# Counts product behind the last tile's heads product, first expert rows ahead of exponentials, and late token rows held back on GpSimd

## The reference

```python
x = x + tanh(g_xattn[0]) * L0_xattn(layernorm(x), ctx)      # 16 heads of 8
x = x + tanh(g_ffn[0])   * L0_ffn(layernorm(x))             # 8 experts, best 2 of each token
x = x + tanh(g_xattn[1]) * L1_xattn(layernorm(x), ctx)
x = x + tanh(g_ffn[1])   * L1_ffn(layernorm(x))             # quantized

def L0_ffn(x):
    probs = softmax(x @ router_w.T)
    topk_probs, topk_idx = top_k(probs, 2)                  # normalised to sum 1
    h = gelu(x @ w_fc[e] + b_fc[e])                         # for each chosen expert e
    y = sum over the two of topk_probs * (h @ w_proj[e] + b_proj[e])
```

## Time and profile before

| | us |
|---|---|
| median of 3 runs | 860.49 |
| lowest, highest run | 856.09, 864.86 |
| profiled execution, its device time | 855.35 |
| its span, first to last instruction | 853.6 |

### The profile page before, as it was taken

The page is one execution under the profiler, slowest core; times in us unless marked ns, Lnnn a source line. Parts: engine busy times, 40 slices in busy tenths (PEclk is TensorE's granted clock), DMA queues, the critical chain, the costliest instruction groups (busy, mean ns, idle before and its releaser), DMA issues. The chain is left out here.

```text
span 853.6 us, 19514 instructions
## 1 busy us (share of the span) xinstructions
PE 696.7 (82%) x6608; PEld 539.2 (63%) x6608; DVE 720.7 (84%) x1821; ACT 595.1 (70%) x1210; POOL 580.8 (68%) x561
## 2 busy tenths in 40 slices
PE   5988879999999989898989989999926879256535
PEld 2767657787877767776768777777723657122234
DVE  3999998989898999776998777778736999799988
ACT  4667657777877766477767767777746888399856
POOL 4675458888888788855577777765558992388810
PEclk9899989999999999799999999999966999666659
DMA  9421812323334122835697877878749622000005
GB/s 247 129 101 54 149 70 97 118 89 116 111 113 144 53 101 102 270 104 187 213 298 236 286 256 270 264 261 276 240 138 303 207 89 74 16 0 1 0 28 170
DMA packets 89665, 127.66 MB, mean 150 GB/s; under 512 B 19888, under 2 KB 64512, under 8 KB 83424
## 3 DMA queue, kind: packets, MB, share of 16 engines
q1 hardware_dynamic: 80016, 108.00, 39.9%
q0 software_dynamic: 8672, 17.99, 6.0%
q10 hardware_dynamic: 880, 0.43, 0.2%
HBM read 82.76 MB, written 43.53 MB: 148 GB/s over the span
## 5 line engine op out<-in xcount | busy, mean ns | idle before, releaser
L531 POOL DMA_INDIRECT m_results<-a_probs,e_to x142 | 147.1, 1036 | 58.0 <-issue 36.3
L521 POOL DMA_INDIRECT m_tokens_to<-r_rows,r_place x128 | 132.2, 1033 | 51.0 <-issue 31.2
L540 POOL TENSOR_TENSOR a_probs<-a_probs,a_top 128x1024 f32<-128x1024 f32 x64 | 122.1, 1908 | 55.3 <-DVE a_top L1512 54.5
L750 ACT ACTIVATE room<-a_ps_s,e_bias 128x512 f32<-128x512 f32 (+1 forms) x160 | 102.0, 646 | 52.6 <-PE a_ps_s L1053 47.2
L658 ACT ACTIVATE a_probs_t<-a_ps_pt 128x512 f32<-128x512 f32 x128 | 69.2, 591 | 65.4 <-PE a_ps_pt L956 65.4
L1542 DVE TENSOR_TENSOR e_hp<-room,e_hp 128x512 fp32r<-128x512 f32 (+1 forms) x160 | 103.2, 645 | 5.5
L1540 DVE CAST e_hp<-room 128x512 fp32r<-128x512 f32 (+1 forms) x160 | 67.7, 423 | 42.1 <-ACT room L750 29.6
L1477 DVE TENSOR_TENSOR a_probs<-a_ps_s,a_mask 128x1024 f32<-128x1024 f32 x64 | 77.9, 1217 | 7.1 <-PE a_ps_s L841 6.6
L940 PEld LDWEIGHTS a_ps_o<-a_vals,a_probs_t 128*64 128x64 f32 x2048 | 66.4, 139 | 21.1 <-issue 20.4
L1512 DVE TENSOR_REDUCE a_top<-a_probs 128x16 f32<-128x1024 f32 x64 | 77.2, 1206 | 0.2
L1049 PE MATMUL a_ps_s<-e_xt,e_weights 128*128 128x512 f32 (+1 forms) x160 | 65.2, 407 | 10.7 <-DMA e_weights<-m_weights_to 10.7
(11 more groups left out here) (366 smaller groups left out, 1928.2 us busy)
## 6 DMA issues: line engine op xcount, KB each, us to landing
e_weights<-m_weights_to SPq DMA_DIRECT2D x40, 1024.0 KB, 4.9
m_weights_to<-r_parts SPq DMA_DIRECT2D x8, 1024.0 KB, 5.7
room<-m_tokens_to SPq DMA_DIRECT2D x31, 264.0 KB, 4.1
c_two<-m_results SPq DMA_DIRECT2D x3, 1536.0 KB, 12.0
a_ctx_in<-in_ctx_dram SPq DMA_DIRECT2D x17, 256.0 KB, 3.7
m_keys_t<-n_keys SPq DMA_DIRECT2D x16, 256.0 KB, 2.2
m_values<-n_values SPq DMA_DIRECT2D x16, 256.0 KB, 3.0
out_dram<-x_sb SPq DMA_DIRECT2D x15, 256.0 KB, 2.3
```

The lines of the kernel that those rows point to most:

```text
L521: pool.indirect_dma_start(tokens_to, bass.IndirectOffsetOnAxis(ap=place[:, k, q:q + 1], axis=0), rows[:, c % RING, q % CT, k, :], None).th ...
L531: pool.indirect_dma_start(results, bass.IndirectOffsetOnAxis(ap=to[:, v, r:r + 1], axis=0), y[:, v, r], None).then_inc(returned[v], 16)
L540: pool.tensor_tensor(probs[:, j], probs[:, j], top[:, j].unsqueeze(2).broadcast_to([P, HEADS, SEQ]), ALU.subtract).then_inc(shifted, 1)
L750: act.activation(h[:, c, at], ps_h[c][:, at], ACT.Gelu_apprx_tanh, bias=bias[:, n % ROWS, c:c + 1]).then_inc(h_sb, 1)
```

## The change

Three moves, with no instruction added or taken away. On PE, `counts(6)` goes from ahead of the heads product of step 65 to ahead of that of step 66, behind all four quarters of `part(-1, ...)`; the wait for `placed` goes to the router of super 14. On ACT, `expert_rows(0)` and the exponentials of step 65 go ahead of `second_weights(6)`; on DVE `expert_rest(0)` goes up, the statistics and `spreads(14)` go from step 64 to step 65, and `take_counts`, `places` and `gates` of chunk 6 go from step 65 to step 66. On POOL, the 12 scatters of q = 40 to 45 leave the attention loop's last six steps: 4 go ahead of `powers(14)` and 8 behind `renumber(7)`.

```diff
--- before.py
+++ after.py
@@ -555,11 +555,13 @@
                 c = s // 2 - 1
                 if j == 0 and s % 2 == 0 and RING <= c < NCH:
                     renumber(c)
-                if t >= SCATTER_LAG:
+                if SCATTER_LAG <= t < SCATTER_LAG + EARLY_CHUNKS * CT:
                     send_rows(t - SCATTER_LAG)
+        for q in range(EARLY_CHUNKS * CT, EARLY_CHUNKS * CT + 2):
+            send_rows(q)
         powers(SUPERS - 2)
         renumber(NCH - 1)
-        for q in range(TILES - SCATTER_LAG, TILES - 2 * CT):
+        for q in range(EARLY_CHUNKS * CT + 2, TILES - 2 * CT):
             send_rows(q)
         paced = 0
         for q in range(TILES - 2 * CT, TILES - CT - QUAD):
@@ -774,10 +776,10 @@
 
         exponentials(TAIL, 0)
         copy_heads(TAIL)
+        expert_rows(0)
+
+        exponentials(TAIL + 1, 1)
         second_weights(NCH - 2)
-        expert_rows(0)
-
-        exponentials(TAIL + 1, 1)
         gelu(0, 0)
         expert_rows(1)
         copy_heads(TAIL + 1)
@@ -1105,7 +1107,6 @@
         t = TAIL + 1
         turn_free(t)
         pe.wait_ge(l_sb, SUPERS - 2)
-        counts(NCH - 2)
         heads_product(t)
         probs_transposes(t)
         pe.wait_ge(s_sb, TILES)
@@ -1116,7 +1117,7 @@
 
         t = TAIL + 2
         turn_free(t)
-        pe.wait_ge(placed, PLACE_OPS * (NCH - 2) + 2)
+        counts(NCH - 2)
         heads_product(t)
         pe.wait_ge(pt_sb, 2 * TILES)
         part(0, 0)
@@ -1133,6 +1134,7 @@
         part(1, 0)
         part(1, 1)
         pe.wait_ge(y_sb, TILES)
+        pe.wait_ge(placed, PLACE_OPS * (NCH - 2) + 2)
         router(SUPERS - 2)
         part(1, 2)
         part(1, 3)
@@ -1564,28 +1566,28 @@
         residual(t)
         first_choice(NCH - 2)
         second_choice(NCH - 2)
+        expert_rest(0)
+
+        t = TAIL + 1
+        reciprocals(t)
+        head_sums(t)
+        residual(t)
+        x_stats(t - 6)
+        spreads(SUPERS - 2)
         x_stats(t - 5)
-        spreads(SUPERS - 2)
-        expert_rest(0)
-
-        t = TAIL + 1
+        split(0, 0)
+        row_offsets(SUPERS - 2)
+        expert_rest(1)
+        for c in range(1, CHUNKS):
+            split(0, c)
+
+        t = TAIL + 2
         reciprocals(t)
         take_counts(NCH - 2)
         head_sums(t)
         residual(t)
-        x_stats(t - 5)
-        row_offsets(SUPERS - 2)
         places(NCH - 2)
         gates(NCH - 2)
-        split(0, 0)
-        expert_rest(1)
-        for c in range(1, CHUNKS):
-            split(0, c)
-
-        t = TAIL + 2
-        reciprocals(t)
-        head_sums(t)
-        residual(t)
         x_stats(t - 5)
         split(1, 0)
         expert_rest(2)
```

More of the change, by code:

```diff
@@ L776, in _ @@
         copy_heads(TAIL)
-        second_weights(NCH - 2)
         expert_rows(0)
         exponentials(TAIL + 1, 1)
+        second_weights(NCH - 2)
         gelu(0, 0)
@@ L1572, in _ @@
         reciprocals(t)
-        take_counts(NCH - 2)
         head_sums(t)
         residual(t)
+        x_stats(t - 6)
+        spreads(SUPERS - 2)
         x_stats(t - 5)
+        split(0, 0)
         row_offsets(SUPERS - 2)
-        places(NCH - 2)
-        gates(NCH - 2)
-        split(0, 0)
         expert_rest(1)
@@ L1586, in _ @@
         reciprocals(t)
+        take_counts(NCH - 2)
         head_sums(t)
         residual(t)
+        places(NCH - 2)
+        gates(NCH - 2)
         x_stats(t - 5)
```

## The result

| | before | changed |
|---|---|---|
| median of 22 runs, us | 856.34 | 864.06 |
| lowest, highest run | 848.94, 864.86 | 858.36, 876.36 |
| profiled execution, span | 853.6 | 860.2 |
| ratio, with its 95% interval | | 1.0093 [1.0071, 1.0115] |

The change costs 8.0 us (0.0093 of 856.34; 6.1 to 9.8): slower, just inside the 1% that the prediction set as its bound. The ratio leaves out executions over 1.5% above the fastest of their kernel, so it differs a little from that of the two medians, which lie 7.7 us apart. The experiments were made in four sessions, each with runs of the kernel before beside it.

The account below looks back on a forecast made before the run. No engine bounds the whole; waits bound the stretch from attention to experts. Second root 6.9 us later, less ACT's 1.0, gives +5.9: 855.35 to 861.3 us profiled, 866.4 from the median 860.49; range 858 to 873.

Parts of the forecast that it names:

- the 1% that the prediction set as its bound: About what a measurement of this kernel can tell from no change, 8.6 us; chance 0.77 within it, 0.19 slower.
- Heads product: PE, step 65: starts at 356.1 instead of 357.88, no longer behind the counts product; a gain of 1.8 us.
- First root: POOL's `spreads(14)`, now behind the reciprocal of step 65: at 360.3 instead of 358.24, 2.0 us later.
- Twenty scatters: POOL between the two roots: 20 scatters instead of 12, at 1.30 us each, take 26.0 us with all waits filled.
- the prediction's bounds: POOL's scatters at 1.26 or 1.40 us each, so 25.2 to 28.0 us for the twenty.
- Second root: POOL's root of super 15: at 388.0 instead of 381.07, 6.9 us later.
- The step to PE: DVE passes on 6.9 us, ACT's slack takes off 1.0; PE's down product of tile 2 comes 5.9 later than 386.56.
- What follows: Behind PE's down product at 392 us: no slack returns the 5.9 us, so the delay is found again at 620 us.
- The clock behind the long stand: Rival, slower past the bound: scatters at 1.40 us plus 1.2 us for PE's lower clock; +9.1, 869.6 us; chance 0.16.
- made up again: Rival: the delay gives weight loads room, returning up to PE's 3.5 us of waits; +2.4, 862.9 us; chance 0.12.
- The gain at the counts product: Rival: PE's gain near 356 us stays and POOL's delay is hidden; -1.8, 858.7 us; chance 0.08.
- The closing chain's 13%: Read as covering only the last few hundred microseconds of the span, saying nothing of the place that the change touches.

Follow-up runs that it names:

- GpSimd's part alone: The kernel before with only POOL's new order, four scatters in the loop and twenty between the roots: +5.9 us beside before at 858.72, +11.1 beside 904.79.
- root first: The changed kernel with super tile 15's root ahead of the twelve late scatters: +2.7 us beside before at 858.72, +21.3 beside 904.79, +14.6 beside 903.89.
- the base of 857: The kernel before, unchanged, in the sessions where its median was 856.34 and 858.72 us; in the other sessions it took 904 to 910 us.

## Why the prediction came out as it did

The direction held, and every step of the chain up to the second root and PE's stand was found in the profile. The place of the root carries about 5 of the 8.0 us in the medians; that the rest comes by the same path is not shown. The sizes, step by step:

- **Heads product.** Forecast 356.1, measured 356.12. But PE gained more than the 1.8 us: the fourth weight load is 3.3 us early. The granted clock is 1.00 from 357 us on, where it read 0.50 from 359 to 361 in the earlier trace rows. The prediction read that 0.50 as following the 2 us wait for `chosen`, but the level had fallen earlier: from 353 to 355 us the windows read 0.65 in before and 0.54 in the change. What differs is the way back to the upper level, which before reached only behind 363 us (0.79 from 363 to 365). GpSimd's part alone, with PE's old order, read 0.50 from 359 to 367; root first, with the new order, 1.00 from 349 to 371. So the shorter stretch goes with the new order in four profiles; that the removed wait is what makes it is argued. The step counted the wait and not the clock. It changed nothing in the end, since PE only stood longer: 10.0 us, forecast some 9.
- **First root.** Forecast 360.3, measured 359.38: the reciprocal began 0.9 us sooner than worked out, behind a heads product of 1.30 us instead of 1.90.
- **Twenty scatters.** Forecast 26.0 us, measured 386.93 - 361.08 = 25.85, with no wait in them. The starts from 361.08 to 378.38, most of them beside DVE's splits, lie 1.33 us apart (13 intervals), those from there to 385.95, nearly all with DVE idle, 1.26 (six). The Trainium skill's rule of the shared SBUF interfaces (GPSIMD Engine Reference, section Specifications) agrees with this trace in its sign; in size it is 0.07 us a scatter, 5%, half of the 0.14 between the prediction's bounds. Not every scatter beside splits is dearer: from 363.91 to 370.23 they took 1.26 or 1.27, and splits beside them 0.54 and 0.77 us instead of 0.42 and 0.69, so there the extra time shows on DVE's side. In the profile of GpSimd's part alone 20 scatters, also beside splits, took (388.32 - 362.94) / 20 = 1.27.
- **Second root.** Forecast 388.0, measured 386.93, all of it the first root's 0.9 us and rounding.
- **The step to PE.** Forecast 5.9 us, measured 391.20 - 386.56 = 4.64 (4.4 by the sixth weight load). ACT's slack of 1.0 us was as worked out: DVE's offset is 5.58 later, ACT's rows 4.62. DVE stood 9.19 us for the root, forecast 7 to 8, since it too was ahead.
- **What follows.** This step failed in size: the prediction let the delay at 392 us stand unchanged to the end. In the profile the delay grows from 4.4 at 400 us to 6.8 at 617. The stretch between the sixth and the last weight load, with the same 1065 matmul records, in before, the change, root first and GpSimd's part alone (columns as in the windows above):

```profile
395.34:610.11 214.77, 199.66 (x1065) 164.59 (x1065) 173.72 (x406) 155.19 (x329) 148.96 (x145) 1.00 0.77 259
...
399.74:616.93 217.19, 203.75 (x1065) 168.28 (x1065) 173.16 (x406) 155.30 (x329) 147.47 (x145) 0.98 0.74 256
...
390.26:606.62 216.36, 200.68 (x1065) 165.67 (x1065) 173.54 (x406) 155.65 (x329) 154.92 (x152) 0.99 0.77 259
...
402.38:620.19 217.81, 199.68 (x1065) 164.73 (x1065) 175.21 (x406) 155.48 (x329) 145.80 (x145) 1.00 0.76 255
```

In the change the 2.4 us are the clock: PE was busy 4.1 us longer for the same products and idle 1.7 us less. The granted clock fell at two places, behind stands of PE for a weight load of 2.02 us (until 436.96) and 2.58 us (until 503.70):

```profile
438.00:440.00 2.00, 2.00 (x12) 1.86 (x10) 1.93 (x4) 1.16 (x2) 1.70 (x2) 0.62 0.93 348
...
504.00:506.00 2.00, 1.99 (x6) 1.41 (x5) 0.00 (x0) 0.56 (x1) 1.39 (x3) 0.50 1.10 389
```

Before's profile reads 1.00 in every window from 392 to 526 us, though PE stood up to 2.1 us there too. Root first, which has no long stand, loses 1.6 us in the same stretch (1.0 of it busy time), and GpSimd's part alone 3.0, all of it idle time. So the growth has no single cause and does not hang on the long stand alone; before's one profile may simply be a good one there. What the 8.0 us of the median hold beyond the 4.4 shown at this place in the trace is open.

- **The rivals.** The clock behind the long stand reads 0.50 until 394 us, but the lower level stood there before too (0.50 from 388 to 390), and the sixth load is no later than the down product: the term of 1.2 us was not seen at this place. A lower clock did cost time further down, as shown, where no rival had put it. Nothing was made up again. The gain at the counts product is not kept.
- **Two readings of the rows.** The closing chain's 13% are 111 us of the span, not the last few hundred. The 0.50 of the earlier trace rows from 359 us does not begin behind the wait of 2 us, as said above.

The sum thus fell short by 2 us (5.9 for 8.0), just outside the interval (6.1 to 9.8). For the profiled execution it gave 861.3 us, and 861.93 was measured; that is in part luck, since a step to PE that was 1.3 too large stands beside a growth of 2.4 that the sum did not have. The forecast of 866.4 us lies 2.3 above the median measured, because it started from a median of 860.49 of three runs that 22 runs put at 856.34: a base 4.2 too high and a loss 2 too low partly cancel, which is luck as well.

## What to carry to other kernels

In an in-order queue, count what stands between two outputs that others wait for, not what the queue's engine has left as idle time: POOL had 4.6 and 2.2 us of waits, was given 10.4 us of work, and the difference, with the first root's 1.1 us on top, came out at PE less ACT's 1.0 us of slack. A small producer (0.2 us) at the end of a run of long instructions is the first thing to move up; here one line gave back about 5 of 8 us on the base of 857, and nothing that could be measured on the slower one. And one profile can show a mechanism while its gain is smaller than the spread between executions: the profile of root first was 3.3 us faster than before's, its median 2.7 slower.

## What was not expected of the hardware

**The same program at two bases.** Before took 856 and 859 us in two sessions and 904 to 910 in three; the number of the chip was the same in the session with 858.72 and in the first of the three, so it alone does not tell them apart. The windows from 450 to 500 us, first before at 853.6, then at 904.3 us of span, show the steady experts:

```profile
450.00:500.00 50.00, 46.26 (x248) 38.49 (x247) 38.14 (x81) 35.86 (x78) 38.67 (x38) 1.00 0.79 274
```

```profile
450.00:500.00 50.00, 44.75 (x208) 36.30 (x207) 36.55 (x87) 29.34 (x61) 30.84 (x31) 0.94 0.70 241
```

PE got 248 matmul records into the one and 208 into the other, at 274 and 241 GB/s. The weight loads, 15 to 30 of the stage, are issued 6.09 us apart in the one (460.80 to 552.18) and 6.98 in the other (489.85 to 594.57). Besides that, engines stand for long times at once without a releaser. In that execution of before at 904.3 us:

```profile
433.40 1.06 PE L1071 MATMUL a_ps<-ident,room 128*128 128x128 f32 x4
...
443.96 0.60 ACT L757 ACTIVATE e_xt<-a_ps 128x512 fp32r<-128x512 f32 x1 [9.14 <-remote]
...
444.65 0.77 PE L1049 MATMUL a_ps_s<-e_xt,e_weights 128*128 128x512 f32 x1 [5.27 <-issue]
```

ACT copies what the transposes made, 9.5 us after they are recorded as done. Whether such records of PE are early, or a signal or a transfer came late, the trace doesn't say; it was not tried.

**A change costs other amounts on the slower base.** GpSimd's part cost 5.9 us on the one and 11.1 on the other, the whole change 8.0 and 14.6, root first 2.7 and 14.6 to 21.3. The ranking of variants on one base did not carry over to the other, and only the base of 857 is the one that the prediction was made for.
